# Second normalisation's row statistics in the attention stage, second quantiser's lower tile on VectorE, FFN operations in three-operand forms

## What is computed

```
h = h + attention(layernorm(h))                     # 12 heads, causal mask, q = k = v
h = h + ffn(layernorm(h))
ffn(z)    = bitlinear(gelu(bitlinear(z, w1, g1)), w2, g2)        # 192 -> 768 -> 192
bitlinear = act_quant(rmsnorm(x) * g) @ weight_quant(w).T
act_quant(x): scale = 127 / max(max|x| of the row, 1e-5);  round(x * scale) clipped / scale
rmsnorm(x): x * rsqrt(mean(x*x) + 1e-6)
```

## Time and profile before

| what | value |
|---|---|
| median of 3 runs | 1921.12 us (1920.8 to 1921.96) |
| the profiled execution, its time | 1918.11 us |
| its span, first to last instruction | 1916.4 us |
| mean granted clock | 0.882 |
| busy share of the span: PE, PEld, DVE, ACT, POOL | 84%, 71%, 72%, 61%, 57% |
| chain that ended last, by engine | PE 70%, DVE 14%, issue 5%, SPq 4%, ACT 3%, DMA 2%, POOL 1% |

### The profile page before, as it was taken

One profiled execution on the slowest core, in us unless ns is written; L12 is line 12 of the kernel. 1 busy time (PEld: TensorE's weight loads), 2 busy tenths in 40 slices (PEclk: granted clock), 3 DMA queues, 4 the chain that ended last, 5 costly groups with the idle time before them and its releaser, 6 DMA issues.

```text
span 1916.4 us, 50514 instructions
## 1 busy us (share of the span) xinstructions
PE 1614.7 (84%) x16574; PEld 1363.0 (71%) x16574; DVE 1371.2 (72%) x3151; ACT 1171.3 (61%) x1830; POOL 1089.9 (57%) x1503
## 2 busy tenths in 40 slices
PE   0539999999999999999999999999556666666666
PEld 0438888888888888888888888887445555555555
DVE  3635666666666666666666666666289999999996
ACT  1124555555555555555555555555278888888887
POOL 5035555555555555555555555554177777777775
PEclk9969999999999999999999999999666666666665
DMA  8564656565656565656565656561000000000000
GB/s 103 137 116 69 100 78 99 79 100 78 100 79 100 78 99 80 100 79 99 80 100 78 99 80 100 79 99 26 24 12 22 22 22 22 22 22 22 22 22 26
DMA packets 159967, 132.96 MB, mean 69 GB/s; under 512 B 32558, under 2 KB 151040, under 8 KB 159808
## 3 DMA queue, kind: packets, MB, share of 16 engines
q1 hardware_dynamic: 159168, 131.00, 44.0%
q0 software_dynamic: 768, 1.57, 0.5%
HBM read 118.32 MB, written 11.91 MB: 68 GB/s over the span
## 4 chain that ended last, share of the span: by engine, by line
PE 70%; DVE 14%; issue 5%; SPq 4%; ACT 3%; DMA 2%; POOL 1%; DVEq 1%; ACTq 0%; POOLq 0%
PE ps L1072 24%; PE ps L1154 8%; PE ps L1237 7%; PE ps L1228 7%; DVE ff_st L857 4%; PE ps L1184 4%; PE ps L1216 3%; PE ps L1189 3%; PE ps L1210 3%; PE ps L1314 3%; PE ps L1333 2%; DVE xpix L838 2%; PE ps L1145 2%; PE ps L1135 1%; PE ps L1168 1%
## 5 line engine op out<-in xcount | busy, mean ns | idle before, releaser
L1072 PE MATMUL ps<-w_eff,xpix 118*112 118x193 f32 (+1 forms) x2048 | 457.2, 362 | 21.0 <-POOL side L438 20.4
L1072 PEld LDWEIGHTS ps<-w_eff,xpix 118*112 118x112 f32 (+1 forms) x2048 | 387.8, 253 | 39.8 <-issue 32.8
L915 ACT ACTIVATE probs<-ps,isw 116x688 f32<-116x688 f32 x384 | 298.7, 830 | 175.6 <-PE ps L1216 175.6
L449 POOL TENSOR_TENSOR xsq<-xsq 118x784 f32<-118x784 f32 (+2 forms) x192 | 221.8, 1155 | 293.6 <-ACT xsq L909 283.5
L738 DVE TENSOR_REDUCE nmax<-ps 116x12 bf16<-116x1344 f32 (+2 forms) x192 | 302.2, 1574 | 108.7 <-PE ps L1189 103.8
L524 POOL TENSOR_TENSOR xpix<-probs,g_b 112x192 f32<-112x192 f32 (+1 forms) x512 | 296.5, 609 | 109.0 <-ACT probs L1024 99.7
L469 POOL TENSOR_SCALAR_AFFINE_SELECT probs<-probs 116x464 f32<-116x464 f32 x384 | 268.4, 717 | 46.5 <-ACT probs L915 31.0
L682 DVE TENSOR_SCALAR front_st<-ps 112x1 f32<-112x1 f32 (+1 forms) x128 | 18.3, 152 | 229.2 <-PE ps L1135 218.1
L1314 PE MATMUL ps<-w1t,xpix 96*112 96x384 f16 (+1 forms) x512 | 160.7, 488 | 14.5 <-ACT xpix L1015 13.3
L1154 PE MATMUL ps<-xnT,wq_pad 97*128 97x228 f32 (+1 forms) x768 | 166.0, 365 | 0.0
L1303 PE MATMUL ps<-ident_h,xpix 112*96 112x112 f16 (+1 forms) x256 | 34.9, 281 | 152.9 <-DVE xpix L874 152.9
(11 more groups left out here) (160 smaller groups left out, 3393.3 us busy)
## 6 DMA issues: line engine op xcount, KB each, us to landing
xpix<-in_x SPq DMA_DIRECT2D x192, 196.0 KB
xpix<-in_x SPq DMA_DIRECT2D x192, 195.1 KB
rden<-den_rows SPq DMA_DIRECT2D x256, 85.5 KB, 2.2
out<-xpix SPq DMA_DIRECT2D x64, 87.0 KB
out<-xpix SPq DMA_DIRECT2D x64, 84.0 KB
xpix<-in_x SPq DMA_DIRECT2D x128, 34.1 KB
xpix<-in_x SPq DMA_DIRECT2D x128, 34.0 KB
den<-o_sb SPq DMA_DIRECT2D x256, 2.7 KB
```

The costliest lines, as they stand in the source:

```text
L449: nc.gpsimd.tensor_tensor(out_, a, b, ALU.add).then_inc(s_ssq, 1)
L915: A(probs[0:TB, g, 2 * e:2 * e + 2, :], ps[0:TB, 4 + 2 * e:6 + 2 * e, 0:SK], ACT.Exp, scale=isw[0:TB, 7:8]).then_inc(s_p, 1)
L1072: last = MM(ps_tok[tile][0:P, :], src, w_eff[0:HI, o, :], start=(o == 0), stop=(o == OFFS - 1))
```

## The change

In the attention stage DVE gets a new last part of its step, `measure(n-1)`, directly behind the third round of maxima: mean and variance of the finished rows, the centred rows, and their peaks, kept for all images in `mean2` and `peak`. POOL takes the root (`row_roots`, kept in `rms`) one step later, behind the third clearing and ahead of `add_squares`. Between the stages DVE works out the first quantiser's scales of all 64 images at once, 128 columns wide. The FFN stage then has no statistics of h. It computes v1 again from the stored mean (`centre`), and every scale operation is two columns wide. ACT quantises only the upper tile of the second rows, DVE the lower one, in one operation 768 elements wide. POOL works out the gelu mean squares' epsilon and root itself, behind the weighting of the same image. DVE's FFN operations that had one tensor and two scalars (tensor_scalar) become scalar_tensor_tensor, with a tensor of constants in SBUF (`magic`, `unit`) as the second tensor. `v1` gets a buffer of its own. The squares are scaled by 768**-0.5 on ACT, so that no division by 768 is needed.

```
@@ buffers, setup
-        ln_st = sb("ln_st", [128, 32])
+        ln_st = sb("ln_st", [128, 40])
+        mean2, rms, peak, inv_peak, step1, scale1: each sb([128, IMAGES * 2]); magic = sb([128, 1])
+        unit = ones[:, 0:2]
-        v1 = part(xpix[0][:, :], 384, 2 * DIM)...
+        v1 = sb("v1", [128, 2, DIM])
+            for filled in (mean2, rms, peak):                       # in DVE's setup
+                step(V.memset(filled[:, :], 1.0))
+            step(V.memset(magic[:, :], MAGIC16))
@@ POOL, attention stage
+            def row_roots(m):
+                pool.wait_ge(s_var2, m + 1)
+                nc.gpsimd.tensor_tensor(rms[:, bass.ds(m * 2, 2)], ln_st[:, 32:34], expo[:, 0:2],
+                                        ALU.pow).then_inc(s_rms, 1)
                 if old:
                     clear_later(n, 2)
+                if prev:
+                    row_roots(n - 2)
                 if newest:
                     add_squares(n + 3)
@@ POOL, FFN stage (replaces ffn_step)
+            def weight(n, b):
+                after(pool, f_q2[0], n - 1)
+                after(pool, f_q2[1], n - 1)
+                for tile, P in enumerate((TA, TB)):
+                    pool.wait_ge(f_g, 2 * n + tile + 1)
+                    ... (the same four multiplications by g2 as before)
+            def gelu_roots(n, b):
+                pool.wait_ge(f_ssq, 2 * n + 2)
+                apart(pool)
+                nc.gpsimd.tensor_scalar(ff_st[:, b, 18:20], gel_sum[:, b, :], EPS_RMS, None,
+                                        ALU.add).then_inc(f_var, 1)
+                pool.wait_ge(f_var, n + 1)
+                nc.gpsimd.tensor_tensor(ff_st[:, b, 20:22], ff_st[:, b, 18:20], expo[:, 0:2],
+                                        ALU.pow).then_inc(f_r1, 1)
@@ DVE, attention stage
+            def measure(n):
+                def chain(ins, k):
+                    ins.then_inc(s_mean2, 1)
+                    dve.wait_ge(s_mean2, n * 3 + k)
+                dve.wait_ge(s_h2, n + 1)
+                apart(dve)
+                for tile, P in enumerate((TA, TB)):
+                    last = V.bn_stats(ln_st[0:P, 20 + 6 * tile:26 + 6 * tile], h_all[0:P, hcols(n, tile)])
+                chain(last, 1)
+                apart(dve)
+                for tile, P in enumerate((TA, TB)):
+                    last = V.bn_aggr(ln_st[0:P, 34 + 2 * tile:36 + 2 * tile], ln_st[0:P, 20 + 6 * tile:26 + 6 * tile])
+                chain(last, 2)
+                after(dve, s_rms, n)
+                V.tensor_scalar(ln_st[:, 32:34], ln_st[:, 35:38:2], 1.0 + EPS_RMS,
+                                EPS_LN * EPS_RMS, ALU.mult, ALU.add).then_inc(s_var2, 1)
+                V.tensor_copy(mean2[:, bass.ds(n * 2, 2)], ln_st[:, 34:38:2])
+                for tile, P in enumerate((TA, TB)):
+                    last = V.scalar_tensor_tensor(v1[0:P, tile, :], h_all[0:P, hcols(n, tile)],
+                                                  ln_st[0:P, 34 + 2 * tile:35 + 2 * tile], g1_b[0:P, :],
+                                                  ALU.subtract, ALU.mult)
+                chain(last, 3)
+                for tile, P in enumerate((TA, TB)):
+                    last = V.tensor_reduce(peak[0:P, bass.ds(n * 2 + tile, 1)], v1[0:P, tile, :], AX_X, ALU.max,
+                                           apply_absolute_value=True)
+                last.then_inc(s_peak, 1)
                 if new:
                     maxima(n + 1, 2)
+                if prev:
+                    measure(n - 1)
@@ DVE, between the stages (waits for all peaks and roots; each link waits for its own result)
+            link(V.tensor_tensor(peak[:, :], rms[:, :], peak[:, :], ALU.mult))
+            link(V.tensor_scalar(peak[:, :], peak[:, :], 1e-5, None, ALU.max))
+            link(V.reciprocal(inv_peak[:, :], peak[:, :]))
+            V.tensor_scalar(step1[:, :], peak[:, :], isw[:, 4:5], None, ALU.mult)
+            link(V.scalar_tensor_tensor(scale1[:, :], inv_peak[:, :], 127.0, rms[:, :], ALU.mult, ALU.mult))
@@ DVE, FFN stage: ffn_step(i, b) now runs, in this order
+   centre(i + 1):           2 x scalar_tensor_tensor v1 <- h_all, mean2, g1_b
+   final(i - 3, 1 - b):     2 x scalar_tensor_tensor y <- ps, ff_st, h_all      (as before)
+   peaks(i - 1, 1 - b):     2 x tensor_reduce of v2, 768 wide, one link         (as before)
+   quantise_first(i + 1):   2 x scalar_tensor_tensor q1 <- v1, scale1, magic broadcast
+   second_scales(i - 1, 1 - b):
+                flink(V.scalar_tensor_tensor(st[:, 28:30], st[:, 20:22], 1.0, st[:, 26:28], ALU.mult, ALU.mult))
+                flink(V.scalar_tensor_tensor(st[:, 28:30], st[:, 28:30], 1e-5, unit, ALU.max, ALU.mult))
+                flink(V.reciprocal(st[:, 32:34], st[:, 28:30]))
+                V.scalar_tensor_tensor(st[:, 42:44], st[:, 28:30], isw[:, 5:6], unit, ALU.mult, ALU.mult)
+                V.scalar_tensor_tensor(st[:, 38:40], st[:, 32:34], 127.0, st[:, 20:22], ALU.mult, ALU.mult)
+   quantise_second(i - 1, 1 - b):
+                dve.wait_ge(f_sc, n + 1)
+                after(dve, f_t2, n)
+                V.scalar_tensor_tensor(q2[0:TB, 1, :], v2[0:TB, b, 1, :], ff_st[0:TB, b, 39:40],
+                                       magic[0:TB, :].to_broadcast([TB, HIDDEN]), ALU.mult, ALU.add)
@@ ACT, FFN stage
-            def quantise(i, b, tile): ... (both tiles)
+            def quantise(n, b): ... (the upper tile alone)
-                          scale=ff_st[0:P, b, 40 + tile:41 + tile]).then_inc(f_g, 1)
+                          scale=step1[0:P, bass.ds(m * 2 + tile, 1)]).then_inc(f_g, 1)
@@ PE, FFN stage, turn_second: one wait for each tile
-                pe.wait_ge(f_q2, n + 1)
+                    pe.wait_ge(f_q2[tile], n + 1)
```

More of the change, by code:

```diff
@@ L238, in build @@
         f_v2 = sem("gelu_weighted")
-        f_q2 = sem("second_quantised")
+        f_q2 = [sem(f"second_quantised{i}") for i in range(2)]
         f_t2 = sem("second_transposed")
@@ L506, in _ @@
             step_images(IMAGES - 1, 0, None, newer=False, newest=False)
[L508 to L534, removed]
+            row_roots(IMAGES - 2)
+            row_roots(IMAGES - 1)
+            def weight(n, b):
[3 more added lines that the diff above has]
+                    pool.wait_ge(f_g, 2 * n + tile + 1)
+                    for lo in range(0, HIDDEN, HIDDEN // 4):
+                        cols = slice(lo, lo + HIDDEN // 4)
+                        last = nc.gpsimd.tensor_tensor(v2[0:P, b, tile, cols], gel[0:P, b, tile, cols],
+                                                       g2_b[0:P, cols], ALU.mult)
+                    last.then_inc(f_v2, 1)
@@ L535, in _ @@
+            gelu_roots(0, 0)
+            weight(1, 1)
+            gelu_roots(1, 1)
+            with pool.Fori(1, PAIRS) as t:
                 for b in range(2):
[L536 to L539, removed]
+                    weight(2 * t + b, b)
+                    gelu_roots(2 * t + b, b)
         @block.vector
@@ new lines, in centre, with quantise_first @@
+            def centre(n):
+                after(dve, f_q1, n)
+                for tile, P in enumerate((TA, TB)):
+                    ins = V.scalar_tensor_tensor(v1[0:P, tile, :], h_all[0:P, hcols(n, tile)],
+                                                 mean2[0:P, bass.ds(n * 2 + tile, 1)], g1_b[0:P, :],
+                                                 ALU.subtract, ALU.mult)
+                ins.then_inc(f_v1, 1)
+            def quantise_first(n):
+                dve.wait_ge(f_v1, n + 1)
+                after(dve, f_t1, n)
+                for tile, P in enumerate((TA, TB)):
+                    ins = V.scalar_tensor_tensor(q1[0:P, tile, :], v1[0:P, tile, :],
+                                                 scale1[0:P, bass.ds(n * 2 + tile, 1)],
+                                                 magic[0:P, :].to_broadcast([P, DIM]), ALU.mult, ALU.add)
+                ins.then_inc(f_q1, 1)
@@ new lines, in final, with peaks @@
+            def final(n, b):
+                dve.wait_ge(f_m2, n + 1)
+                after(dve, f_out, 32 * n)
+                for tile, P in enumerate((TA, TB)):
+                    end = V.scalar_tensor_tensor(y[0:P, tile, :], ps[0:P, 1, tile * 256:tile * 256 + DIM],
+                                                 ff_st[0:P, b, 42 + tile:43 + tile], h_all[0:P, hcols(n, tile)],
+                                                 ALU.mult, ALU.add)
+                end.then_inc(f_y, 1)
+            def peaks(n, b):
+                dve.wait_ge(f_v2, 2 * n + 2)
+                for tile, P in enumerate((TA, TB)):
+                    ins = V.tensor_reduce(ff_st[0:P, b, 26 + tile:27 + tile], v2[0:P, b, tile, :], AX_X, ALU.max,
+                                          apply_absolute_value=True)
+                flinks[:] = [0, n * F_LINKS]
+                flink(ins)
@@ L888, in _ @@
             ffn_step(IMAGES - 1, 1, new=False)
[L889 removed]
+            ffn_step(IMAGES, 0, new=False)
```

135 lines of the change are left out of this document (53 added, 82 removed).

## The result

| kernel | median, us | from, to | runs |
|---|---|---|---|
| before | 1919.51 | 1915.25 to 1924.73 | 20 |
| after | 1913.49 | 1902.57 to 1919.49 | 20 |

The ratio is 0.9971 (0.996 to 0.9982): 0.3% faster, where 1.8% was forecast, and 1.5 us above the range's upper end. The profiled execution took 1913.02 us, its span 1911.2, at a mean granted clock of 0.912.

The account below looks back on a forecast made before the run. PE was taken to bound attention, DVE the FFN stage. DVE's step falling from 7.95 to 7.4 us over 63 steps saves 34.7, attention and ends 0: 1883.4 us profiled, 3.0 more for the median, 1886; range 1858 to 1912.

Parts of the forecast that it names:

- the term of the first quantiser: FFN stage, DVE: change in the first quantiser's time including waits for POOL, -0.1 to 0.64 us a step, taken 0.2.
- the other three terms: FFN stage, DVE: waits added at the centring (0.25 us), the scales (0.15) and the 768-wide second quantiser (0.25) per step.
- centring: FFN stage, DVE: waits for POOL added to both centring halves, 0 to 0.76 us a step, taken 0.25.
- scales: FFN stage, DVE: change in the scale operations with waits, -0.2 to 0.55 us a step, taken 0.15.
- 768 wide: FFN stage, DVE: second quantiser's lower tile, 0.92 us of new work plus 0 to 0.38 of waits, taken 0.25.
- `measure`: Attention stage, DVE: new part takes 3.2 us (bounds 2.8 to 4.4), fits the 3.38 us hole and costs nothing.
- Ends: Between the stages +1.6 us, at the end of the kernel about -1.6; net 0, within 2 us.
- POOL and ACT: FFN stage: POOL's step 7.3 us, nearly level with DVE's; ACT 6.9 us with waits, not binding at 7.4.
- ACT did not bind: Rival, FFN stage: POOL and DVE hardly collide, ACT's 6.9 us sets the step, 1855 us; chance 0.19.
- `measure` did not grow: Rival, attention stage: `measure` takes 4.1 to 4.4 us and delays PE, 1899 to 1918 us; chance 0.09.
- The forms give everything back: Rival, FFN stage: added DVE waits of 1.4 us or more cancel the gain, step 8.15, 1934 us; chance 0.10.
- what finds it idle doesn't wait: Argument for limiting that slower case: at an 8.88 us step POOL would idle 1.6 us, sparing DVE operations waits.

Follow-up runs that it names:

- e4: Changed kernel with POOL's wait for its own upper-tile result put back ahead of the lower tile's blocks: 1881.85 us, 0.9804.
- e7: Kernel before with POOL's wait between the two tiles taken out: 2011.85 us, 1.0477.
- e8: Changed kernel with POOL's stop between the tiles and both tiles of the second quantiser on ACT: 1852.52 us, 0.9657.
- e10: Changed kernel with POOL's stop between the tiles, short DVE forms and both second-quantiser tiles on ACT: 1852.67 us, 0.9656.
- e2: Changed kernel, no stop, with all DVE three-operand forms with a constant turned back to the short forms: 1915.38 us, 0.9986.
- e3: Changed kernel with DVE's constant operands in a PSUM bank only DVE uses, PE's first transposes moved to banks 6 and 7: 1882.96 us, 0.9819.
- e14: Changed kernel with POOL's only added stop behind the second block of the lower tile: 1907.86 us, 0.9933.
- e1: Changed kernel with the first quantiser alone back as tensor_scalar: 1898.41 us, 0.9888.
- e13: Changed kernel with POOL's only added stop behind the second block of the upper tile: 1877.93 us, 0.9781.
- e6: Changed kernel, no stop, with constants, peaks and scales in PSUM, so no FFN-step DVE operation reads two SBUF tensors: 1853.57 us, 0.965.
- e11: Changed kernel with POOL waiting for its own result behind every block of the weighting: 1902.92 us, 0.992.
- e9: Changed kernel with POOL's stop between the tiles and DVE's three-operand forms with a constant turned back to short ones: 1848.39 us, 0.9629.

## Why the prediction was wrong

**The step that failed** is the term of the first quantiser, "-0.1 to 0.64 ... taken 0.2", and behind it the diff's reading on POOL, "the same four multiplications". They are the same, but the wait between the tiles is gone, and the prediction gave it no price. It counted waits for one block at a time; without the stop one operation waits for up to four. The term measured 0.82, above even its upper bound: the first half went from 573 to 1290 ns, the second from 307 to 406. That is 0.62 a step more than taken, 39 us over 63 steps; the other three terms came out 0.16 lower in sum and give 10 back. The forecast was 27.5 us short. With the stop back (e4) the same term is (652 - 573) + (406 - 307) = 0.18 us, the step 7.39, and the time 1881.85: the forecast of 7.4 and 1886 is that kernel's. Its four terms are 0.18, 0.22 (centring), 0.09 (scales) and 0.32 (768 wide), 0.81 in sum where 0.85 was taken.

The two-by-two says it once more (us): long forms without a stop 1913, with it 1882; short forms 1915 and 1848. The change took away a stop worth 31 to 67 us, and e7 shows that it was worth 93 to the kernel before.

**The other terms of the added waits** lay within their bounds: centring 584 + 409 against 518 + 406 ns is 0.07 (taken 0.25), the scales' five operations 1.65 against 1.44 is 0.21 (0.15), the 768-wide operation 1.133 against 0.92 is 0.21 (0.25). Sum of all four 1.31, and 6.55 + 1.31 = 7.86 for a measured 7.92.

**`measure`** was right. It fills the hole between the third maxima and `front` in the timeline of DVE:

```profile
800.45 1.11 DVE L760 TENSOR_REDUCE nmax<-ps 116x4 bf16<-116x912 f32 x1
801.48 0.61 DVE L788 BATCH_NORM_STATS2 ln_st<-h_all 112x6 f32 x2
...
802.52 0.58 DVE L795 TENSOR_SCALAR ln_st<-ln_st 128x2 f32<-128x2 f32 x1
...
803.09 0.73 DVE L799 SCALAR_TENSOR_TENSOR v<-h_all,ln_st,g_b 112x192 f32<-112x192 f32 x2
803.95 0.61 DVE L804 TENSOR_REDUCE peak<-v 112x192 f32 x2
804.97 0.16 DVE L704 TENSOR_SCALAR front_st<-ps 112x1 f32<-112x1 f32 x1 [0.41 <-PE ps L1192]
```

From 801.48 to 804.56 are 3.08 us (forecast 3.2). 16.8 us in 42 waits, 0.40 each, are left of the earlier trace rows's 3.38:

```profile
DVE front_st L704 <- PE ps L1192: 16.8, 42, 0.4
```

PE is busy 799.72 of 800 us and the stage ends no later, so it didn't grow, and POOL's root (681 ns) cost nothing.

**Ends**: the start grew from 4.56 to 6.65 us (+2.1, forecast +1.6), the end shrank from 19.1 to 17.3 (-1.8, forecast -1.6).

**POOL and ACT**: epsilon's addition takes 217 ns (taken 350), the root 876 (690), the blocks 0.72 on the mean against 0.608. Without its wait for gelu, 49.4 us in 44 steps, POOL's step is 7.92 - 1.12 = 6.8 us, below the 7.3 expected. ACT waits in the changed kernel; it bound only in e8 and e10.

**The rivals.** ACT did not bind at 7.92. `measure` did not grow. "The forms give everything back" named the right place, the operations behind the gelu peaks while POOL weights, and nearly the right sum. But e2 says that it is not the forms: back in their short form, without the stop, nothing is won. Its argument, "what finds it idle doesn't wait", failed outright in e7: POOL is idle for 38% of the stretch, yet the step is the longest of all, and DVE comes to its scales just when POOL has begun.

The Trainium skill's page "SBUF — State Buffer" (section "Who interferes with whom") has the contention between VectorE with two SBUF inputs and GpSimd, and a loser blocked for the whole of the other's instruction. The runs agree on the operands: the same operation takes 414 ns with its constant in PSUM (e3) and 1290 with it in SBUF. By that rule a loser waits for one instruction, 0.6 us at most here; the measured 2600 ns are four. Nor does the number of SBUF inputs explain by itself that the short form waits as long in e2.

**What stays open.** Long waits need a POOL that nothing stops soon: a stop of its own (e4) or a gelu not yet done (after, e7) keeps them away, and those that did wait were let in with one to three blocks left before POOL's next wait (after, e14). It is no strict rule: in e1 15 requests in the third and fourth block went in within it, though the gelu was done and no stop ahead. Whether POOL's instructions already handed out go first, or DVE's request loses each new race until the queue drains, no run here tells apart. e13, made for it, had no request in the place that mattered.

## What to carry to other kernels

A wait that looks idle may be what lets another engine in: before you drop a semaphore wait inside a long run of GpSimd instructions, look in the timeline for VectorE operations that start beside them, and price the whole run, not one instruction of it. When the same operation takes three times as long in its first tile as in its second, read the other engines' rows at that moment, before its form is blamed. Look too at which of GpSimd's other waits are already fulfilled when it comes to them: such a wait stops nothing. Where the wait can't be had, operands of VectorE in a PSUM bank of its own do as well, if all of its operations there are treated so (e6); the constants alone brought half of that gain (e3).

## What the runs showed of the hardware

- A VectorE operation of 0.41 us with its tensors in SBUF was held up for up to 2.6 us by GpSimd multiplications of 0.59 us issued back to back (after), one of 0.16 us for 2.48 (e7). One stop of 0.21 us among eight of them limits it to one (757 ns at most in 350 us, e4); a stop behind every block costs more than it gives (1902.92 us, e11).
- In the changed kernel all 33 first halves that asked after the second gelu's end waited through two to four blocks, and none of the 29 that asked before it. While that wait of GpSimd's was still unfulfilled, VectorE was let in within the block.
- The forms with one tensor and scalars wait as long (1900 ns in e2) as those with two tensors. With the second in PSUM no long wait is left (408 to 418 ns, e3 and e6), and GpSimd's blocks take 591 instead of 792 ns (lower tile).
- Blocks of 384 columns take 1.01 to 1.04 us on GpSimd, of 192 columns 0.59; the longer ones hold DVE up by more (1873 against 1848 us).
- The granted clock in the FFN stage was 0.65 before, 0.76 after at nearly the same step (7.97 and 7.92 us), 0.76 in e8 and 0.87 in e9. PE never set the pace there, and no run tried what the clock alone is worth.
